# An attention and mixture-of-experts layer on one core: constant, maxima and hidden layer on other engines, finer first loads

## The reference

```
q, k, v = layernorm(x) @ W_attn + b_attn          # 16 heads of 8
q, k = elu(q) + 1, elu(k) + 1
step t: kv += k_t (x) v_t ; ksum += k_t ; y_t = (q_t . kv) / (q_t . ksum + 1e-6)
x = x + y @ W_proj + b_proj
z = layernorm(x)
p = softmax(z @ Wr + br) ; keep the top 2 of 8 experts, divide by their sum
x = x + sum_e p_e * (relu(z @ W1_e + b1_e) @ W2_e + b2_e)     # hidden size 512
```

## Time and profile before

| | us |
|---|---|
| median of 3 runs | 440.23 |
| lowest and highest of them | 438.25 and 440.63 |
| the profiled execution | 439.78 |
| its span, first to last instruction | 438.0 |

### The profile page before, as it was taken

The page is one execution under the profiler, slowest core; times in us unless marked ns, Lnnn a source line. Parts: engine busy times, 40 slices in busy tenths (PEclk is TensorE's granted clock), DMA queues, the critical chain, the costliest instruction groups (busy, mean ns, idle before and its releaser), DMA issues.

```text
span 438.0 us, 8095 instructions
## 1 busy us (share of the span) xinstructions
PE 312.8 (71%) x2488; PEld 243.6 (56%) x2488; DVE 324.4 (74%) x698; ACT 170.0 (39%) x346; POOL 261.8 (60%) x247
## 2 busy tenths in 40 slices
PE   0499894987888879879642205979989987989400
PEld 0388663654665656657332104868778876878400
DVE  4488967999778988999972633876777865878357
ACT  0488408650410411421304003545446553556153
POOL 1635816999537887887757750455556553656700
PEclk9999996996998998999855556999999998999955
DMA  7970000000000100000111112222222222221188
GB/s 207 319 204 2 2 0 1 0 2 0 0 0 8 36 32 17 33 26 25 43 42 38 55 43 73 63 75 75 74 75 75 77 71 69 72 69 53 43 323 257
DMA packets 24045, 29.38 MB, mean 67 GB/s; under 512 B 3803, under 2 KB 18659, under 8 KB 24006
## 3 DMA queue, kind: packets, MB, share of 16 engines
q1 hardware_dynamic: 18566, 18.99, 14.9%
q0 software_dynamic: 4544, 9.38, 6.5%
q10 hardware_dynamic: 896, 0.50, 0.5%
HBM read 16.19 MB, written 12.67 MB: 66 GB/s over the span
## 4 chain that ended last, share of the span: by engine, by line
PE 27%; DVE 22%; issue 19%; POOL 18%; DMA 7%; ACT 6%; SPq 1%; POOLq 0%; ACTq 0%; DVEq 0%
POOL y_rows L491 14%; PE ps L1066 8%; DVE nd L794 5%; PE ps L1065 4%; POOL x_rows L450 3%; DVE work L788 2%; DMA y_rows<-wraw,yid 2%; DMA qk<-y_rows 2%; ACT xs L572 2%; PE ps L1039 2%; DVE wm L721 2%; PE ps L1087 2%; PE ps L1123 1%; DVE y_s L805 1%; DVE rd L801 1%
## 5 line engine op out<-in xcount | busy, mean ns | idle before, releaser
L491 POOL DMA_INDIRECT y_rows<-wraw,yid x78 | 81.4, 1044 | 74.4 <-ACT wraw L633 61.0
L1066 PE MATMUL ps<-kvt,tri 128*128 128x384 f32 (+1 forms) x192 | 73.2, 495 | 13.8 <-DVE work L788 12.0
L420 POOL TENSOR_TENSOR kvt<-qk,v 128x1024 f32<-128x1024 f32 x32 | 67.4, 2129 | 20.3 <-DVEq L883 7.8
L450 POOL DMA_INDIRECT x_rows<-rows,pos_i x64 | 62.6, 978 | 27.7 <-issue 17.3
L966 DVE TENSOR_TENSOR wraw<-ps,b1s 128x1024 f32<-128x1024 f32 x39 | 47.8, 1224 | 22.5 <-PE ps L1216 19.6
L1230 PE MATMUL ps<-w,wraw 128*128 x312 | 55.9, 222 | 8.4 <-DVE wraw L974 8.3
L1066 PEld LDWEIGHTS ps<-kvt,tri 128*128 128x128 f32 x192 | 38.4, 207 | 35.6 <-issue 20.4
L1231 PE MATMUL ps<-w,wraw 128*128 x312 | 55.4, 222 | 0.0
L1232 PE MATMUL ps<-w,wraw 128*128 x312 | 55.4, 221 | 0.0
L1214 PE MATMUL ps<-wraw,w1h 128*128 128x256 f16 x156 | 43.3, 277 | 7.7 <-ACT wraw L621 5.8
L788 DVE TENSOR_TENSOR work<-ps,qk 128x1152 f32<-128x1152 f32 x32 | 42.4, 1352 | 7.9 <-PE ps L1070 7.6
(11 more groups left out here) (198 smaller groups left out, 648.2 us busy)
## 6 DMA issues: line engine op xcount, KB each, us to landing
wraw<-x_rows SPq DMA_DIRECT2D x39, 130.0 KB, 2.1
qk<-y_rows SPq DMA_DIRECT2D x8, 512.0 KB, 6.8
x<-in_L_attn_x_dram SPq DMA_DIRECT2D x4, 512.0 KB, 9.6
wraw<-in_L_ffn_W_dram SPq DMA_DIRECT2D x1, 2048.0 KB, 12.4
out_dram<-x SPq DMA_DIRECT2D x8, 256.0 KB, 4.5
y_rows<-wraw,yid POOLq DMA_INDIRECT x78, 2.4
x_rows<-empty SPq DMA_DIRECT2D x9, 130.0 KB, 4.5
x_rows<-rows,pos_i POOLq DMA_INDIRECT x64, 2.3
```

Source lines behind the costliest of these rows:

```text
L420: nc.gpsimd.tensor_tensor(kvt[:, u % RING, a].rearrange("p (j h i) -> p j h i", j=DH, i=DH), k.unsqueeze(1).broadcast_to([P, DH, H, DH]), ...
L450: nc.gpsimd.indirect_dma_start(out=x_rows, out_offset=bass.IndirectOffsetOnAxis(ap=pos_i[:, c, t:t + 1], axis=0), in_=rows[:, t, :], in_of ...
L491: nc.gpsimd.indirect_dma_start(out=y_rows, in_=ysb[:, n % XG, g], in_offset=None, out_offset=bass.IndirectOffsetOnAxis(ap=yid[:, n % XG, g ...
L1066: nc.tensor.matmul(o, tri[:, :], kv[a][:, cols], start=(a == 0), stop=True)
```

## The change

Four edits:

1. The addition of the constant to the denominators moves from DVE to ACT (`denominator`); ACT's casts of weights move behind the copies of a step, and DVE's statistics move behind the reductions.
2. In the inner layer ACT adds the hidden bias and applies relu straight from PSUM, in four activations per block (`hidden`, into `hid`), DVE rounds to fp16 (`hidden_high`) and forms the remainder (`hidden_low`). PE starts with the output bias for both halves at once, then all products of the high part, then those of the low part. The rings of x blocks and results have 6 places, and `yid` has one for every block; DVE no longer waits for a scatter.
3. The maxima over partitions are no longer an all-reduce on POOL: PE transposes the three columns, DVE reduces them and spreads them over a diagonal, PE multiplies with ones.
4. x is loaded in five pieces of 2, 6, 8, 8 and 8 tiles, and DVE takes the statistics of the first two before it splits the bias. `add_bproj` for later quarters moves behind the first two `kv_products` on POOL; PE's projection waits for its own quarter.

```diff
-    LOADS = 4
-    TPL = NT // LOADS
-    UPL = TPL // TPU
+    LN_TILES = [0, 2, 8, 16, 24, 32]
+    LOADS = len(LN_TILES) - 1
+    TPB = 8
...
-    XG = 4
+    XG = 6
...
-        yid = sb("yid", [P, XG, GPB], I32)
+        yid = sb("yid", [P, NBLK, GPB], I32)
...
+            nc.gpsimd.memset(den_eps[:], DEN_EPS).then_inc(const_done, 1)
...
             layer_norm_1(0)
             layer_norm_1(1)
+            layer_norm_1(2)
...
-            layer_norm_1(2)
-            add_bproj(0)
-            layer_norm_1(3)
-            for g in range(1, LOADS):
-                add_bproj(g)
...
+            layer_norm_1(3)
+            add_bproj(0)
+            layer_norm_1(4)
             kv_products(0)
             kv_products(1)
-            pool.wait_ge(wmax_done, 3)
-            nc.gpsimd.partition_all_reduce(sc[:, 4:7], sc[:, 0:3], P, bass.bass_isa.ReduceOp.max).then_inc(wall_done, 1)
+            add_bproj(1)
+            add_bproj(2)
+            add_bproj(3)
             pool.wait_ge(empty_out, 16 * (E + 1))
...
+            def denominator(u):
+
+                par = u % 2
+                act.wait_ge(red_done, (u + 1) * TPU)
+                if u >= 2:
+                    act.wait_ge(y_done, u - 1)
+                nc.scalar.activation(rd[:, par], nd[:, par].rearrange("p a (j h) -> p a j h", j=NPL)[:, :, DH, :], ACT.Identity,
+                                     bias=den_eps[:, :]).then_inc(den_done, 1)
...
-            act.wait_ge(scale_done, 1)
-            nc.scalar.activation(b1s[:], b1T[:], ACT.Copy, scale=sc[:, 17:18]).then_inc(b1s_done, 1)
             for s in range(U):
                 if s - 3 in ended_by:
                     copy_x2T(ended_by[s - 3])
-                if s < E // W_CHUNK:
-                    for e in range(s * W_CHUNK, (s + 1) * W_CHUNK):
-                        cast_weights(e)
+                denominator(s)
                 if s - 3 in ended_by:
                     copy_logits(ended_by[s - 3])
                 copy_yT(s)
                 copy_x2(s)
+                if s == 0:
+                    act.wait_ge(scale_done, 1)
+                    nc.scalar.activation(b1s[:], b1T[:], ACT.Copy, scale=sc[:, 17:18]).then_inc(b1s_done, 1)
+                if s < E // W_CHUNK:
+                    for e in range(s * W_CHUNK, (s + 1) * W_CHUNK):
+                        cast_weights(e)
                 if s - 2 in ended_by:
                     norm_2(ended_by[s - 2])
...
-            def hidden_high(n):
-                act.wait_ge(pre_done, n + 1)
+            PER = 13
+            regs = [act.alloc_register(name=f"act_expert{j}") for j in range(PER)]
+
+            def hidden(n):
+
+                if n % PER == 0:
+                    act.load(regs, table_i[0:1, 1, n:n + PER])
+                act.wait_ge(up_done, n + 1)
                 if n >= 2:
-                    act.wait_ge(down_done, n - 1)
-                nc.scalar.activation(hh[:, n % 2], pre[:, n % 2], ACT.Relu).then_inc(hi_done, 1)
+                    act.wait_ge(lo_done, n - 1)
+                e = act.snap(regs[n % PER], min_val=0, max_val=E - 1)
+                for c in range(HC):
+                    at = c % 2 * SLOTS
+                    ins = nc.scalar.activation(hid[:, n % 2, c], ps[:, 2 + 2 * (n % 2) + c // 2, at:at + SLOTS], ACT.Relu,
+                                               bias=b1s[:, bass.ds(e * HC + c, 1)])
+                ins.then_inc(hid_done, 1)
...
+            for g in range(2):
+                dve.wait_ge(x_in[g], 16)
+                stats(LN_TILES[g], LN_TILES[g + 1])
+                group_moments(g)
+
             dve.wait_ge(small_in[0], 16)
             link(nc.vector.tensor_scalar(bias_in[:, 0:2 * D], bias_in[:, 0:2 * D], 1.0, None, ALU.add))
...
+            def maxima_over_partitions():
+                dve.wait_ge(maxT_done, 1)
+                link(nc.vector.tensor_reduce(max3[:, 0:1], ps[0:3, 6, T:T + P], AX.X, ALU.max))
+                nc.vector.tensor_scalar(max3[:, 1:4], ident[0:3, 0:3], max3[:, 0:1], None, ALU.mult).then_inc(max3_done, 1)
...
-                link(nc.vector.tensor_scalar(rd[:, par], ndp[:, :, DH, :], DEN_EPS, None, ALU.add))
+                dve.wait_ge(den_done, s + 1)
                 link(nc.vector.reciprocal(rd[:, par], rd[:, par]))
...
+            maxima_over_partitions()
             for s in range(U):
                 for a in range(TPU):
                     multiply(s, a)
+                    if s == 0 and a == 0:
+                        dve.wait_ge(wall_done, 1)
+                        link(nc.vector.tensor_copy(sc[:, 4:7], ps[:, 6, T + P:T + P + 3]))
+                reduce(s, 0)
+                reduce(s, 1)
                 if s >= 1:
                     statistics(s - 1)
-                reduce(s, 0)
-                reduce(s, 1)
                 quotient(s)
...
+            def hidden_high(n):
+                dve.wait_ge(hid_done, n + 1)
                 if n >= 2:
-                    dve.wait_ge(lo_done, n - 1)
...
+                    dve.wait_ge(down_done, n - 1)
+                nc.vector.tensor_copy(hh[:, n % 2], hid[:, n % 2]).then_inc(hi_done, 1)
 
             def hidden_low(n):
                 dve.wait_ge(hi_done, n + 1)
-                if n >= 2:
-                    dve.wait_ge(down_done, n - 1)
-                nc.vector.scalar_tensor_tensor(out=hl[:, n % 2], in0=pre[:, n % 2], scalar=0.0, in1=hh[:, n % 2],
-                                               op0=ALU.max, op1=ALU.subtract).then_inc(lo_done, 1)
+                nc.vector.tensor_tensor(hl[:, n % 2], hid[:, n % 2], hh[:, n % 2], ALU.subtract).then_inc(lo_done, 1)
 
             def y_rows_of(n):
                 dve.wait_ge(loaded[n % XG], 16 * (n // XG + 1))
-                if n >= XG:
-                    dve.wait_ge(y_scattered[n % XG], 16 * GPB * ((n - XG) // XG + 1))
...
             def proj(u):
                 if u >= 1:
                     pe.wait_ge(x2_done, u)
+                pe.wait_ge(xb_done, u * TPU // TPB + 1)
...
-            pe.wait_ge(xb_done, LOADS)
+            pe.wait_ge(wmax_done, 2)
+            nc.tensor.transpose(ps[0:3, 6, T:T + P], sc[:, 0:3], ident[:, :]).then_inc(maxT_done, 1)
             prefix(0, 0)
+            pe.wait_ge(max3_done, 1)
+            nc.tensor.matmul(ps[:, 6, T + P:T + P + 3], ones[0:3, :], max3[:, 1:4], start=True, stop=True).then_inc(wall_done, 1)
             prefix(0, 1)
...
+                both = ps[:, 6 + n % 2, 0:GPB * D].rearrange("p (g d) -> p g d", g=GPB)
+                nc.tensor.matmul(both, ones3[:, :], b2p[:, bass.ds(e, 1), :].broadcast_to([3, GPB, D]), start=True, stop=False)
...
+                pe.wait_ge(hi_done, n + 1)
+                for g, o in enumerate(outs):
+                    for c in range(HC):
+                        h = hh[:, n % 2, c, g * P:(g + 1) * P]
+                        nc.tensor.matmul(o, h, high[c], start=False, stop=False)
+                        nc.tensor.matmul(o, h, low[c], start=False, stop=False)
                 pe.wait_ge(lo_done, n + 1)
...
                 for g, o in enumerate(outs):
...
+                    for c in range(HC):
+                        ins = nc.tensor.matmul(o, hl[:, n % 2, c, g * P:(g + 1) * P], high[c], start=False,
+                                               stop=(g == GPB - 1 and c == HC - 1))
                 ins.then_inc(down_done, 1)
```

119 lines of the change are left out of this document (53 added, 66 removed).

## The result

| | before | changed |
|---|---|---|
| median, us | 440.25 | 423.74 |
| lowest and highest of four runs | 438.25, 440.63 | 420.66, 424.39 |
| profiled execution | 439.78 | 424.10 |
| its span | 438.02 | 421.84 |

A forecast was written before the change was run, and what follows sets the result against it. No engine was full throughout: DVE, PE and POOL shared the scan, PE with stalls bound the inner layer. Gains 1.4 + 4 + 6.5 + 9.5 = 21.4 took 439.78 to 418.4, 419 on the median's scale; range 410 to 430.

The forecast's parts named there:

- Head: Start of kernel: loop starts 3.2 us earlier, first prefix loses 1.8 waiting for the maxima; net 1.4 us gained.
- beside the second prefix: Head: the later small product and small DVE instructions lie beside the second prefix, costing 0.2 us each if not.
- Steps 0 and 1: First scan steps: no all-reduce on POOL and an earlier ACT copy of y gain 4 us, between 2.6 and 6.0.
- Constant and statistics: Scan steps 4 to 15: constant on ACT (2 kept) and statistics behind reductions (4.5 kept) gain 6.5 us together.
- POOL becomes the limit: Scan steps 8 to 13: POOL's busy time and gaps make 59 to 62 of 62.7 us, allowing 3.6 at most.
- Inner layer: Blocks: fewer stalls (8.0), shorter first chain (0.9) and one wide bias product (0.6) gain 9.5 us; PE stays bound.
- the wait for scatters: Inner layer: DVE's 14.6 us wait for landed scatters goes with a place for every block's numbers; 4.1 us gained.
- First chain: Inner layer: the shorter chain to the first product (1.2 + 1.05 + 1.2 becomes 1.6 + 0.8) gains 0.9 us.
- POOL held by the cast: Inner-layer rival: POOL cannot issue during DVE's cast, 3.3 us a block over PE's 3.15, costing 6 us: 425; chance 0.12.
- the wait that changes owner: Scan rival: ACT's queue holds the constant as long as POOL did; 6.5 becomes 0, step 1's 4 becomes 2.6: 427; chance 0.24.
- ACT as the bound: Inner-layer rival: four activations with register-chosen bias make ACT the bound, 4.2 us a block at 0.85 each: 457; chance 0.06.
- the row at 209.75: Scan profile row: addition took its usual 0.18 behind a scatter's start at 208.84; taken as no loss between cast and scatter.

The follow-up runs named there:

- the run with the constant ahead of the queue: Changed kernel with ACT adding the constant before copies of turned groups, and one expert's casts before it, one behind, in steps 1 to 3: 422.11 us.
- the run with 20 numbers: Changed kernel with PE loading 20 expert numbers at blocks 0 and 20, in place of 8 at five blocks: 445.97 us, ratio 0.9860.
- the last four runs: Changed kernel on other chips: x loads of eight tiles 440.44; 20 expert numbers per load 445.97; reordered engine queues with 20 numbers 440.17, with eight 428.28 us.

## Why the prediction was right, and where it was off

The direction and the three places were right, and the sum was 5 us too high, in five terms.

1. *Head* (1.4 gained predicted, 0.55 lost; by the spread above between 0.9 lost and 1.2 gained, so that its sign is not shown and only the miss is). The loop's start was mis-sized to the safe side: 4.6 for 3.2. The wait of the first prefix for the maxima was right (1.6 for 1.8). The step that failed is the unwritten one behind it: the prefix was taken at its old length. PE had paused 3.2 us, its clock fell, and from its start to the multiply the first prefix took 1.8 us more, the second, with the small product in front of it, 1.4 more (5.18 between the two multiplies for 3.82). The sentence that put the small product "beside the second prefix" was wrong for the same reason: PE runs in order, and the product stood in front.
2. *Steps 0 and 1* (4 predicted). Step 1 did give 4.2; with the all-reduce on POOL again it still gave 2.3 (12.46 for 14.79), so that about half came without the change of the maxima. But steps 2 and 3 lost 3.1, 1.4 of it with the late clock and the rest since the constant waits behind the casts (with the constant on DVE they lose nothing). The prediction saw these waits (1 to 3 us in steps 1 to 4) and put them into its 2 us for the constant, not against this gain.
3. *Constant and statistics* (6.5 predicted for steps 4 to 15; 7.2 measured). The statistics alone were worth 5.2 to 6.7, a little over the 4.5 kept; the constant 0.3 to 1.9 over all steps, for 2 kept, and not to be told from nothing. "POOL becomes the limit" was right in kind: steps 8 to 13 gave 0.9 of the 3.6 allowed. What it missed is the form: the wait for POOL does not go with the addition; the quotient behind it has two inputs in SBUF and waits for the same products.
4. *Inner layer* (9.5 predicted, 8.1 in the table, 7.5 by the run of it alone). Four activations, the cast and the pace were right. The wide bias product gave nothing (pace 3.19 before and after; 0.6 predicted), PE's loads of numbers cost 6.0, in the kernel before 5.5 by the same intervals, ACT's 2.5 for 2. That the wait for scatters leaves the path was right, but the places that were to take it away weren't needed: with rings of four it stays off the path too.
5. *First chain* (0.9 predicted, a part of the 9.5). The stretch from step 15 to the first copy gave 0.8. The run of the inner layer alone can't confirm it, since its clock came back later there.

Three numbers of the working were off without moving the sum by 1 us. PE is busy for all of an undisturbed block's 3.19 in both kernels, not for some 3.15, so that the rival of POOL held by the cast would have cost 4 rather than 6 us. 24 gaps of 0.3 to 0.5 beside POOL's 51.9 make 59.1 to 63.9, not 59 to 62. And 3.45 less 2.4 makes 1.05 for the first chain, not 0.9.

Of the rivals, the wait that changes owner was half true: for the constant, not for the statistics. ACT as the bound fell with 1.57 for four activations. POOL held by the cast fell by its price and not as a mechanism. Timeline of the changed kernel:

```profile
274.34 1.23 DVE L1002 TENSOR_TENSOR wraw<-wraw 128x1024 f16<-128x1024 f32 x1
...
275.10 1.30 POOL L500 DMA_INDIRECT y_rows<-wraw,yid  x1 [0.63 <-ACT wraw L665]
...
290.66 1.25 POOL L500 DMA_INDIRECT y_rows<-wraw,yid  x1 [0.30 <-issue]
291.11 0.69 DVE L998 CAST wraw<-wraw 128x1024 f16<-128x1024 f32 x1 [2.46 <-ACT wraw L657]
```

At 276.70 a scatter's issue keeps its 0.95 with a cast of 0.69 inside, which begins 0.10 behind it. At 290.66 the cast begins 0.45 behind it, and the issue takes 1.25 and ends 0.11 behind the cast. The issue at 275.10, which begins inside the subtraction, takes 1.30. So DVE does hold issues, by 0.3 to 0.4, but the pace of 3.19 stays; the row at 209.75, with an addition 0.91 behind the start of an issue, was no test of it. The Trainium skill, SBUF — State Buffer, "Who interferes with whom", has the rule on which that rival stood; the trace agrees with it at 290.66 and doesn't show it at 276.70. The same section says that a DVE instruction with two inputs in SBUF contends with a GpSimd instruction that reads SBUF; there the trace agrees (4.05 for a quotient of 0.62, in the run with the constant ahead of ACT's queue).

## What to carry to other kernels

A wait laid in front of products of TensorE that are ready can cost more than itself: here 1.6 us of waiting, and 1.8 more on the first prefix at the half clock. Put the products that are ready in front of the wait. When an operation waits for another engine's long instruction, look at the next operation of the same kind before moving it, for the wait may pass to that one. And before buying buffers against a wait, ask who has slack: a wait of 24 us on DVE cost 0.35 in a kernel in which PE sets the pace and DVE has time to spare.

## What the runs showed of the hardware

After pauses of PE of 3.2 and 4.2 us its clock was at the lower level (0.50 from 50 to 54.2 in the changed kernel and from 339 to 344 in the run with 20 numbers; products every 0.21 for 0.11); after one of 1.77 it was not. The Trainium skill, TensorE: Matmul & The Clock Gate, "HAM oscillation — how this bites in real kernels", tells the same of waits for DMAs; here DVE's maxima and a load of registers did it. How much of the work behind the pause of 3.2 ran at the lower level differed by execution (2.48 to 3.62 for the same six products).

A load of 8 expert numbers into PE's registers cost 1.4 to 1.6 us of PE's pace in the changed kernel. One of 20 made intervals 5.2 and 4.2 over the pace in the two runs that have it, part of it clock.

On the chips of the last four runs a copy of a result starts 0.9 to 1.3 us after PE has ended (medians; 1.3 for 335.99 above), on the others 0.04. The only other thing it waits for by the program is the scatter six blocks back, but that is not it: by the packets of the scatters' queue in these traces, that scatter had landed 14 us or more before. In most blocks the copy starts 0.3 to 0.5 us after POOL's second issue for the block before has ended (335.60 for the copy at 335.99); most of these second issues take 1.25 there, with the cast inside them. What sets the pace of 3.5 to 3.6 there stays open.
